# Reordering the seam between the two halves of a linear-attention layer: key copies, the key-value sum and an output block

## The chip, the cores and the metric

The kernel runs on one core of one Trainium2 chip. The metric is the device time of one launch in microseconds (us). The engines are TensorE (PE; its weight loads are shown apart as PEld), VectorE (DVE), ScalarE (ACT), GpSimd (POOL) and SyncE (SP), which here only issues transfers. Each runs its own instruction stream in order, and they meet at semaphores.

## The reference, cut to what matters

Two layers follow each other on `x` of shape (2, 2048, 512). The first is a gated state-space layer (Mamba) and takes the larger part of the time; the change doesn't touch it. The second is a linear attention with a feed-forward end:

```
xn  = layernorm(x)
q   = softmax(xn @ Wq + bq)            over the 64 features of each of 8 heads
k   = softmax(xn @ Wk + bk + mask)     over the 2048 tokens
v   = xn @ Wv + bv
att = sum over tokens of k (outer) v   one 64x64 matrix a head, for each batch row
y   = q @ att
h   = silu(layernorm(y) * (1 + scale) + shift)
out = x + h @ W_out + b_out
```

`att` of a batch row needs all of its keys and values. So nothing of `y` and `out` for the second batch row can be computed until the last block of keys and values of that row has been summed in.

## The kernel before, in words

The second layer works on 16 blocks of 256 tokens (two tiles of 128): blocks 0 to 7 are batch row 0, blocks 8 to 15 are batch row 1. Two pipelines run in one loop `for n in range(16)` that is written out by hand for each engine: the projections of block `n`, and from `n = 9` on also the output of block `K = n - 9` of batch row 0. After the loop the projections are over, and the output of blocks 7 to 15 remains. The stretch around the end of the loop is the one that changes.

The steps and the lines that the profile gives them:

- `q_mm`, `v_mm`, `k_mm`, `o_mm` (TensorE, all L435): products with 32-bit weights split in a high and a low part, 12 matmuls of 512 columns a tile for q, v and o. `o_mm(K)` makes the two tiles 2K and 2K+1 of the last product, called o12 and o13 for `K = 6`.
- `k_tr`, `q_tr` (TensorE, L480, L472): transposes of the exponentiated keys and queries. `k_evac` (ScalarE, 128x512, `arena_c<-ps,keep`) copies the two transposed key tiles out of PSUM with the mask, and `q_evac` (ScalarE, `arena_c<-ps`) the queries.
- `kv_mm(n)` (TensorE, L490, 16 matmuls) is the key-value sum of block n in one PSUM bank; it waits for both copies of `k_evac(n)`. `add_kv(n)` (VectorE, L1163, four instructions) adds it to the running sum and frees the bank. `k_sums` (L1171, L1173, L1175) closes the softmax's denominator, and `attention(1)` (L1184, four instructions) writes the attention matrix of batch row 1.
- `y_mm(K)` (TensorE, L500, two tiles, 16 matmuls). For `K >= 8` it waits for `attention(1)`. `y_block(K)` (VectorE): two scalings out of PSUM (L1196), the statistics (L1083) and their aggregation (L1088). `layer_rs` (GpSimd, L1306 to L1311) makes the scale and offset, `norm_h(K)` (ScalarE, two 128x512, `arena_b<-arena_b`) applies them.
- `h_tr(K)` (TensorE, L429, 8 transposes), `feat_h(K)` (ScalarE: four times a SiLU out of PSUM and a copy to `xh`), `lows` (VectorE, L1099, four subtractions to `xl`), then `o_mm(K)` and `finish(K)` (VectorE, L1208, one addition for each tile). `bias_rows(K)` (GpSimd, L1404) has added the output bias to the residual rows before. SyncE stores the result and loads the residual rows of a later block into the same buffer.

PSUM has 8 banks, given out in turn by `bank8`: each product takes the next bank and first waits until what held it before has been read. In the stretch at hand, by that turn, the banks of the steps are: o12 bank 2 (held before by the first half of `h_tr(6)`), o13 bank 3 (the second half of `h_tr(6)`), `kv_mm(15)` bank 4 (held before by `kv_mm(14)`), the halves of `h_tr(7)` banks 5 and 6 (the transposed keys of block 15), then y16 to y19 banks 7, 0, 1, 2, o14 bank 3 and o15 bank 4.

The feature buffers `xh`/`xl` come in three sets, and `f_bufs`, between SiLU and subtraction, in three.

Of the kernel before, what the change touches and what calls it, by code (L numbers as in the profile page):

```python
# [18 lines left out]
def program(nc, A, out):  # L19
# [12 lines left out]
    with ctx:  # L32
# [185 lines left out]
        def _(e):  # L218
# [135 lines left out]
            for s in range(NS + LAG + 3):  # L354
# [3 lines left out]
                if s < NS:  # L358
# [8 lines left out]
                    if c > 0 and (j, pr) in OUTM:  # L367
                        n, q0 = divmod(OUTM[j, pr], 8)
# [11 lines left out]
                    if (U, pr) in CPART:  # L380
                        i, n = CPART[U, pr]
# [32 lines left out]
            def bank8(key, release):  # L414
                i = order[nxt[0] % len(order)]
                nxt[0] += 1
                if held8[i] is not None:
                    e.wait_ge(*held8[i])
                held8[i] = release
                bank_of[key] = i  # L420
                return PS[i]

            def feat_tr(no, Z):
                for g in range(2):
                    P = bank8(("ft", no, g), (a_f, 4 * no + 2 * g + 2))
                    for q in range(2):
                        for n in range(2):
                            f = 2 * g + q
                            last = e.transpose(P[:, TB * q + 128 * n:TB * q + 128 * n + 128], Z[:, n, 128 * f:128 * f + 128], ident)  # L429
                    last.then_inc(p_ft)  # L430

            def product(P, lhs, rhs):
                for k in range(4):
                    for n, (a, b) in enumerate(((0, 0), (0, 1), (1, 0))):
                        last = e.matmul(P, lhs(a, k), rhs(b, k), start=(k == 0 and n == 0), stop=(k == 3 and n == 2))  # L435
                return last
# [31 lines left out]
            def q_tr(t):  # L468
                e.wait_ge(a_qe, t + 1)
                P = bank8(("qt", t), (a_qT, t + 1))  # L470
                for f in range(4):
                    last = e.transpose(P[:, 128 * f:128 * f + 128], q_bufs[t % 4][:, 128 * f:128 * f + 128], ident)  # L472
                last.then_inc(p_qt)
# [9 lines left out]
            def kv_mm(n):  # L483

                e.wait_ge(a_E, 2 * n + 2)
                e.wait_ge(v_v, 2 * n + 2)
                P = bank8(("kv", n), (v_ac, n + 1))
                for f in range(4):
                    for t in (2 * n, 2 * n + 1):
                        last = e.matmul(P[:, 128 * f:128 * f + 128], E_bufs[t % 4][:, 128 * f:128 * f + 128],  # L490
                                        vv[:, t % 4, 128 * f:128 * f + 128], start=(t % 2 == 0), stop=(t % 2 == 1))
                last.then_inc(p_kv)
# [10 lines left out]
            def h_tr(K):  # L503
                e.wait_ge(a_nx, 2 * h_no(K) + 2)
                feat_tr(h_no(K), x_bufs[2 + K % 2])

            def o_mm(K):
                ht = t_bufs[h_no(K) % 3]
                e.wait_ge(v_lo, 4 * h_no(K) + 4)
                e.wait_ge(v_wl, 8)  # L510
                for n in range(2):
                    P = bank8(("o", 2 * K + n), (v_o, 2 * K + n + 1))
                    product(P, lambda a, kk: ht[a][:, kk, 128 * n:128 * n + 128], W("o")).then_inc(p_o)

# [3 lines left out]
            for n in range(16):  # L518
                K = n - 9
# [24 lines left out]
            k_tr(15)  # L544
            y_mm(7)
            q_tr(31)
            o_mm(6)
            kv_mm(15)
            h_tr(7)
            y_mm(8)  # L550
            y_mm(9)
# [10 lines left out]
        def _(e):  # L562
            def act(o_, i_, f, **kw):
                return e.activation(o_, i_, f, **kw)  # L564
# [246 lines left out]
            def norm_h(K):  # L811
                norm(h_no(K), x_bufs[2 + K % 2])
# [31 lines left out]
            def feat_h(K):  # L844
                b = K // 8
                feat(h_no(K), lambda f: g2[:, f, b:b + 1], lambda f: b2[:, f, b:b + 1], ACT.Silu)
# [5 lines left out]
            def q_evac(t):  # L852
                at_ = 128 * (t % 18)
                e.wait_ge(p_qt, t + 1)
                if t >= 18:
                    e.wait_ge(p_ya, t - 17)
                act(qT[:, :, at_:at_ + 128], PS[bank_of["qt", t]].rearrange("p (a b) -> p a b", a=4), ACT.Identity).then_inc(a_qT)
# [40 lines left out]
            for n in range(16):  # L898
                K = n - 9
# [24 lines left out]
                if K >= 0:  # L924
                    feat_h(K)
                    if n < 15:
                        e.preload_act_table_set("natural_log_exp_and_others")
            norm_h(7)
            k_evac(15)
            q_evac(31)  # L930
            feat_h(7)
            norm_h(8)
            norm_h(9)
# [7 lines left out]
        def _(e):  # L941
# [85 lines left out]
            for s in range(NS):  # L1027
# [10 lines left out]
                if (U, pr) in ((62, 14), (63, 4)):  # L1038
                    n = 2 + U - 62
# [54 lines left out]
            def lows(no):  # L1094
                hi, lo = t_bufs[no % 3]
                for f in range(4):
                    i = 4 * no + f
                    e.wait_ge(a_fh, i + 1)
                    e.tensor_tensor(lo[:, f, :], f_bufs[i % 3], hi[:, f, :].bitcast(f32), SUB).then_inc(v_lo)  # L1099
# [53 lines left out]
            def add_kv(n):  # L1153

                P = PS[bank_of["kv", n]]
                e.wait_ge(p_kv, n + 1)
                if n % 8 == 0:
                    e.tensor_scalar(flat(acc), P, 1.0, None, MUL).then_inc(v_ac)
                else:
                    e.wait_ge(a_fc, n)  # L1160
                    e.wait_ge(v_ac, n)
                    for f in range(4):
                        last = e.scalar_tensor_tensor(acc[:, f, :], acc[:, f, :], fac[:, n, f:f + 1], P[:, 128 * f:128 * f + 128],  # L1163
                                                      MUL, ADD)
                    last.then_inc(v_ac)
# [11 lines left out]
            def attention(b):  # L1177
                e.wait_ge(v_ac, 8 * b + 8)
                e.wait_ge(v_ks, 4 * b + 4)
                e.wait_ge(g_att, 3)  # L1180
                if b:
                    e.wait_ge(p_ya, 16)
                for f in range(4):
                    e.scalar_tensor_tensor(att[:, f, :], acc[:, f, :], ks[:, f:f + 1], bm, MUL, MUL).then_inc(v_att)  # L1184

            def y_block(K):
                yt = x_bufs[2 + K % 2]
                if K >= 2:
                    e.wait_ge(p_ft, 2 * h_no(K - 2) + 2)
                else:  # L1190
                    e.wait_ge(v_wl, 8)
                e.wait_ge(v_rq, 2 * K + 2)
                for n in range(2):
                    t = 2 * K + n
                    e.wait_ge(p_ya, t + 1)
                    e.tensor_tensor(yt[:, n, :].rearrange("p (a b) -> p a b", a=8),  # L1196
                                    PS[bank_of["y", t]].rearrange("p (a b) -> p a b", a=8),
                                    rq[:, t, :].unsqueeze(2).broadcast_to([128, 8, 64]), MUL).then_inc(v_y)
                e.wait_ge(v_y, 2 * K + 2)
                layer_norm(h_no(K), yt)  # L1200

            def finish(K):
                for n in range(2):
                    t = 2 * K + n
                    O = o_bufs[xo_buf(K, n)]
                    e.wait_ge(p_o, t + 1)
                    e.wait_ge(g_xo, t + 1)
                    e.tensor_tensor(O, PS[bank_of["o", t]], O, ADD).then_inc(v_o)  # L1208
# [19 lines left out]
            for n in range(16):  # L1228
                K = n - 9
                if n < 15:  # L1230
                    norm_x(n + 1)
                if n >= 2:
                    add_kv(n - 2)
                if n == 9:
                    attention(0)
                q_part(2 * n)
                v_part(2 * n)
                if n == 8:
                    k_sums(0)
                if K >= 0:  # L1240
                    y_block(K)
                k_part(n, 0)
                if n == 15:
                    k_part(n, 1)
                sum_part(2 * n)
                if K >= 1:
                    finish(K - 1)
                if n < 15:
                    lows(feat_no(n + 1))
                if n == 3:  # L1250
                    for h in range(2):
                        split_o(h)
                q_part(2 * n + 1)
                v_part(2 * n + 1)
                if n < 15:
                    k_part(n, 1)
                sum_part(2 * n + 1)
                if K >= 0:
                    lows(h_no(K))
            add_kv(14)  # L1260
            y_block(7)
            k_sums(1)
            finish(6)
            add_kv(15)
            attention(1)
            lows(h_no(7))
            y_block(8)
            y_block(9)
# [433 lines left out]
```

## Time and profile before

| | us |
|---|---|
| median of 3 runs | 2419.46 (2418.34 to 2419.83) |
| the profiled execution's own time | 2415.44 |
| its span, first to last instruction | 2413.7 |
| TensorE busy | 2229.7 (92%) |
| VectorE busy | 2165.5 (90%) |
| GpSimd busy | 1916.4 (79%) |
| ScalarE busy | 1679.5 (70%) |

Times inside the trace are us from the start of the span. The second layer's projections begin near 1933, its loop ends near 2323 and the last output rows are made near 2410. In a timeline, a row gives start, duration, engine, line, what is written and read, the number of instructions merged in it, and in brackets the engine's idle time before it with what ended that. The ends of matmuls are modelled, so starts are the better measure on TensorE.

### The profile page before, as it was taken

The numbers are of one execution on the slowest core, as the hardware profiler recorded it, in microseconds if no ns is written. First come the engines' busy times: TensorE is split into PE (matmuls) and PEld (weight loads), VectorE is DVE, ScalarE is ACT, GpSimd is POOL, SyncE is SP. The second block draws the span as 40 slices with busy tenths as digits, with TensorE's granted clock in tenths as the row PEclk, the third lists the DMA queues.
The fourth block names the chain that finished last, engine by engine and source line by source line (L and its number), as shares of the span: only waits on it lengthen the run. The fifth ranks groups of instructions, "written<-read, shape, count | busy, mean of one in ns | idle before, by whom it ended". The sixth has DMA issues, their size and how long they took to land. (4 is left out here: it accounts for less than half of the span.)

```text
span 2413.7 us, 24243 instructions
## 1 busy us (share of the span) xinstructions
PE 2229.7 (92%) x6954; PEld 1151.1 (48%) x6954; DVE 2165.5 (90%) x2363; ACT 1679.5 (70%) x3268; POOL 1916.4 (79%) x1250
## 2 busy tenths in 40 slices
PE   9898999989998999899889998998987899999989
PEld 3233334334433443344334333433433388988878
DVE  4898999999999999999999999999999966666666
ACT  3677777877787778778877877787555455466655
POOL 0789999999999999999999999999987722232225
PEclk9999999999999999999999999999998999999999
DMA  6510231032004110411041023003100121011113
GB/s 228 203 61 26 74 132 35 31 131 75 31 31 158 44 35 27 159 57 65 19 174 44 31 75 131 27 31 129 60 31 20 65 77 34 26 56 58 49 53 123
DMA packets 78050, 176.10 MB, mean 73 GB/s; under 512 B 7453, under 2 KB 10781, under 8 KB 77918
## 3 DMA queue, kind: packets, MB, share of 16 engines
q1 hardware_dynamic: 77918, 174.56, 21.4%
q8 instruction: 56, 0.92, 0.1%
q14 instruction: 76, 0.62, 0.1%
HBM read 157.23 MB, written 17.30 MB: 72 GB/s over the span
## 5 line engine op out<-in xcount | busy, mean ns | idle before, releaser
L1379 POOL TENSOR_TENSOR arena<-arena 128x1024 f32<-128x1024 f32 x512 | 1198.9, 2358 | 106.7 <-ACT arena L564 73.5
L984 DVE TENSOR_TENSOR_SCAN arena<-ps,arena 128x512 f32<-128x512 f32 x1024 | 1237.7, 1249 | 0.8 <-ACT ps L564 0.6
L564 ACT ACTIVATE ps<-arena 128x512 f32<-128x512 f32 x1087 | 723.7, 681 | 370.4 <-DVE arena L984 298.2
L307 PE MATMUL ps<-arena,keep 128*128 128x512 f32 x1770 | 861.3, 617 | 119.8 <-POOL arena L1379 91.9
L972 DVE TENSOR_TENSOR arena<-ps,arena 128x1024 f32<-128x1024 f32 x512 | 615.1, 1201 | 19.3 <-PE ps L307 11.7
L307 PEld LDWEIGHTS ps<-arena,keep 128*128 128x128 f32 x1770 | 331.5, 194 | 599.3 <-issue 339.3
L253 PE MATMUL ps<-arena 128*128 128x512 f32 x1024 | 460.4, 593 | 0.7 <-ACT arena L564 0.7
L253 PEld LDWEIGHTS ps<-arena 128*128 128x128 f32 x1024 | 194.6, 191 | 247.8 <-issue 247.3
L564 ACT ACTIVATE arena<-arena 128x2 f32<-128x2 f32 (+2 forms) x599 | 227.5, 383 | 23.5 <-POOL arena L1339 12.2
L293 PE MATMUL ps<-arena 128*128 128x512 f32 x512 | 233.3, 597 | 0.0
L1339 POOL TENSOR_TENSOR arena<-arena 128x512 f32<-128x512 f32 x168 | 213.3, 1271 | 10.1 <-ACT arena L564 2.1
L1384 POOL TENSOR_TENSOR arena<-arena 128x512 f32<-128x512 f32 x139 | 177.3, 1276 | 10.9
L564 ACT ACTIVATE arena<-ps 128x512 f32<-128x512 f32 (+2 forms) x273 | 138.5, 516 | 65.2 <-PE ps L253 22.8
L564 ACT ACTIVATE arena<-ps,keep 128x509 f32<-128x509 f32 (+3 forms) x240 | 167.7, 699 | 22.7 <-PE ps L253 12.5
L1397 POOL TENSOR_TENSOR arena_c<-arena_c 128x512 f32<-128x512 f32 x32 | 33.4, 1044 | 167.2 <-DVE arena_c L1139 166.0
L293 PEld LDWEIGHTS ps<-arena 128*128 128x128 f32 x512 | 98.4, 192 | 124.3 <-issue 124.1
L1306 POOL TENSOR_SCALAR arena_b<-arena_b 128x2 f32<-128x2 f32 x32 | 8.2, 257 | 151.4 <-DVE arena_b L1088 151.3
L564 ACT ACTIVATE arena_c<-arena_c 128x256 f32<-128x256 f32 (+3 forms) x112 | 54.9, 493 | 74.9 <-POOL arena_c L1397 48.4
L303 PE MATMUL ps<-arena 128*128 128x512 f32 x128 | 72.7, 651 | 37.0 <-DVE arena L990 35.9
L564 ACT ACTIVATE arena_b<-ps,keep 128x256 f32<-128x256 f32 x128 | 70.9, 554 | 49.8 <-PE ps L429 40.3
L1099 DVE TENSOR_TENSOR xl<-arena_b,xh 128x256 fp32r<-128x256 f32 x128 | 57.5, 468 | 45.9 <-ACT xh L564 45.1
L1111 DVE SCALAR_TENSOR_TENSOR arena_c<-ps,keep,arena_b 128x256 f32<-128x256 f32 x64 | 28.0, 480 | 65.5 <-PE ps L435 65.5
(146 smaller groups left out, 2697.8 us busy)
## 6 DMA issues: line engine op xcount, KB each, us to landing
arena<-scr_bc SPq DMA_DIRECT2D x128, 512.0 KB, 6.4
arena<-in_inT SPq DMA_DIRECT2D x128, 256.0 KB, 2.6
arena<-in_x SPq DMA_DIRECT2D x17, 512.0 KB, 4.1
scr_x<-arena SPq DMA_DIRECT2D x32, 256.0 KB, 2.0
arena_b<-scr_x SPq DMA_DIRECT2D x16, 512.0 KB, 3.7
arena_c<-scr_x SPq DMA_DIRECT2D x32, 256.0 KB, 2.9
out<-arena_c SPq DMA_DIRECT2D x32, 256.0 KB, 2.0
arena<-in_x SPq DMA_DIRECT2D x30, 256.0 KB, 3.5
```

Source lines behind the costliest of these rows:

```text
L253: last = e.matmul(P, W[:, q, :], xnT[c % 2][:, q, :], start=(q == 0), stop=(q == 3))
L293: e.matmul(P, u[c % 2][:, q, 128 * n:128 * n + 128], wout[:, q, :], start=(c == NCH - 1 and q == 0 or parts and q == 6), stop=(q == 7 or p ...
L303: e.matmul(YP, dg[U % 2], u[c % 2][:, j, :], start=True, stop=False)
L307: last = e.matmul(YP, ident, hb[G % R][:, i, :], start=False, stop=(g == NG - 1 and i == n - 1))
L564: return e.activation(o_, i_, f, **kw)
L972: e.tensor_tensor(hb[G % R], DU.unsqueeze(1).broadcast_to([128, GN, T]), Bt[:, GN * g:GN * g + GN, :], MUL).then_inc(v_tt)
L984: e.tensor_tensor_scan(H, DA[s % 4], H, h0, MUL, ADD).then_inc(v_sc)
L1099: e.tensor_tensor(lo[:, f, :], f_bufs[i % 3], hi[:, f, :].bitcast(f32), SUB).then_inc(v_lo)
L1339: e.tensor_tensor(v, v, tp[:, w, :], ADD).then_inc(g_tap)
L1379: m_ = e.tensor_tensor(H, H, Ct[:, GN * g:GN * g + GN, :], MUL)
L1384: m_ = e.tensor_tensor(H[:, 0, :], H[:, 0, :], H[:, 1, :], ADD)
L1397: e.tensor_tensor(Q3, Q3, m8[t % 4].unsqueeze(2).broadcast_to([128, 8, 64]), SUB).then_inc(g_q)
```

## The change

The arithmetic is the same; four places in the written-out order at the end of the loop differ. TensorE: the key-value sum of block 15 stands between the two tiles of output block 6 and no longer behind both. ScalarE: the copies of the last keys and queries stand ahead of the normalisation of block 7. VectorE: `y_block(7)` comes before `add_kv(14)`, and `finish(6)` comes behind `attention(1)`.

```diff
@@ block.tensor
-            def o_mm(K):
+            def o_mm(K, tiles=(0, 1)):
                 ht = t_bufs[h_no(K) % 3]
                 e.wait_ge(v_lo, 4 * h_no(K) + 4)
                 e.wait_ge(v_wl, 8)
-                for n in range(2):
+                for n in tiles:
                     P = bank8(("o", 2 * K + n), (v_o, 2 * K + n + 1))
@@
             k_tr(15)
             y_mm(7)
             q_tr(31)
-            o_mm(6)
+            o_mm(6, (0,))
             kv_mm(15)
+            o_mm(6, (1,))
             h_tr(7)
             y_mm(8)
             y_mm(9)
@@ block.scalar
-            norm_h(7)
             k_evac(15)
             q_evac(31)
+            norm_h(7)
             feat_h(7)
             norm_h(8)
             norm_h(9)
@@ block.vector
+            y_block(7)
             add_kv(14)
-            y_block(7)
             k_sums(1)
-            finish(6)
             add_kv(15)
             attention(1)
+            finish(6)
             lows(h_no(7))
             y_block(8)
             y_block(9)
```

With the new order on TensorE, `kv_mm(15)` takes bank 3 (held before by the second half of `h_tr(6)`), and o13 takes bank 4 (held before by `kv_mm(14)`).

## Rows read from the trace of the kernel before

**Rows 1.** Waits of TensorE from 2352 on: total us, times, longest us.

```profile
PE ps L435 <- DVE xl L1099: 2.5, 1, 2.5
```

**Rows 2.** The chain that ended last: start us, us, what.

```profile
2339.01 1.29 DVE arena_b L1196 x2
...
2347.13 1.26 ACT arena_b L564 x2
```

**Rows 3.** Timeline of TensorE, 2324 to 2353.

```profile
2324.05 0.50 PE L435 MATMUL ps<-wh_o,xh 128*128 128x512 f32 x1 [0.48 <-DVE xl L1099]
...
2326.95 0.39 PE L435 MATMUL ps<-wh_o,xh 128*128 128x512 f32 x1
...
2332.31 2.05 PE L490 MATMUL ps<-arena_c 128*128 128x128 f32 x16 [2.48 <-ACT arena_c L564]
2334.19 1.04 PE L429 MATMUL ps<-keep,arena_b 128*128 128x128 f32 x8
2336.75 3.84 PE L500 MATMUL ps<-arena_c 128*128 128x128 f32 x32 [1.52 <-DVE arena_c L1184]
...
2345.91 1.04 PE L429 MATMUL ps<-keep,arena_b 128*128 128x128 f32 x8
...
2352.10 0.50 PE L435 MATMUL ps<-wh_o,xh 128*128 128x512 f32 x1 [2.50 <-DVE xl L1099]
```

**Rows 4.** Timeline of TensorE: `kv_mm(13)`, then the first matmuls of q30 and v30.

```profile
2290.09 1.95 PE L490 MATMUL ps<-arena_c 128*128 128x128 f32 x16
2291.79 0.48 PE L435 MATMUL ps<-wh_q,xh 128*128 128x512 f32 x1
...
2294.63 0.39 PE L435 MATMUL ps<-wh_v,xh 128*128 128x512 f32 x1
```

**Rows 5.** Timeline of ScalarE, 2329 to 2348.

```profile
2329.59 1.52 ACT L564 ACTIVATE arena_b<-arena_b 128x512 f32<-128x512 f32 x2 [6.05 <-POOL arena_b L1311]
2331.01 1.24 ACT L564 ACTIVATE arena_c<-ps,keep 128x512 f32<-128x512 f32 x2
2332.15 0.59 ACT L564 ACTIVATE arena_c<-ps 128x512 f32<-128x512 f32 x1
...
2346.41 1.52 ACT L564 ACTIVATE arena_b<-arena_b 128x512 f32<-128x512 f32 x2 [1.24 <-POOL arena_b L1311]
```

**Rows 6.** Timeline of VectorE, 2323 to 2339.

```profile
2323.91 1.11 DVE L1163 SCALAR_TENSOR_TENSOR arena_c<-arena_c,ps 128x128 f32<-128x128 f32 x4
2324.95 1.28 DVE L1196 TENSOR_TENSOR arena_b<-ps,arena_c 128x512 f32<-128x512 f32 x2
...
2327.75 0.16 DVE L1171 TENSOR_TENSOR arena_c<-arena_c 128x32 f32<-128x32 f32 x1
...
2334.39 1.12 DVE L1163 SCALAR_TENSOR_TENSOR arena_c<-arena_c,ps 128x128 f32<-128x128 f32 x4 [3.84 <-PE ps L490]
2335.55 1.14 DVE L1184 SCALAR_TENSOR_TENSOR arena_c<-arena_c 128x128 f32<-128x128 f32 x4
...
2338.66 0.42 DVE L1099 TENSOR_TENSOR xl<-arena_b,xh 128x256 fp32r<-128x256 f32 x1 [0.48 <-ACT xh L564]
```

**Rows 7.** Timeline of GpSimd: `bias_rows(7)`.

```profile
2329.51 2.50 POOL L1404 TENSOR_TENSOR arena_c<-arena_c,arena_b 128x512 f32<-128x512 f32 x2
```

**Rows 8.** A later `bias_rows` on GpSimd and a subtraction of `lows` beside it.

```profile
2364.22 2.70 POOL L1404 TENSOR_TENSOR arena_c<-arena_c,arena_b 128x512 f32<-128x512 f32 x2
...
2364.54 1.26 DVE L1099 TENSOR_TENSOR xl<-arena_b,xh 128x256 fp32r<-128x256 f32 x1 [0.41 <-ACT xh L564]
```

**Rows 9.** Timeline of TensorE, first layer: four matmuls behind a stall, twice.

```profile
209.53 1.98 PE L307 MATMUL ps<-arena,keep 128*128 128x512 f32 x4 [2.96 <-POOL arena L1379]
...
232.17 3.48 PE L307 MATMUL ps<-arena,keep 128*128 128x512 f32 x4 [2.66 <-POOL arena L1379]
```

**Rows 10.** Windows there: stretch, length, PE busy, granted clock, DMA share, GB/s.

```profile
209.50:212.50 3.00, 2.98 (x7) 1.00 0.02 5
...
232.20:235.60 3.40, 3.40 (x5) 0.56 0.00 0
```

## The prediction

> **What bounds the kernel now.** I read the windows of equal length first, to find the stretch that the change touches, then the waits of TensorE, the chain that ended last, and the timeline of each engine from 2320 to 2352. In the second layer TensorE is the engine that sets the time: from 2352 to the end its list of waits has one entry, the 2.5 us that ends at 2352.10 [rows 1], and behind it stands nothing but its own work. So the time of the whole kernel follows the start of the matmuls at 2352.10, the first tile of output block 8 (o16). Whatever moves that start moves the end by as much. The question is what sets it.
>
> The timeline of TensorE shows three long stalls ahead of that point [rows 3]: 2.48 us before `kv_mm(15)` (until 2332.31), 1.52 us before `y_mm(8)` (until 2336.75), and 2.50 us before o16. The reader should see that the third isn't caused by anything near it. Back from 2352.10 the chain goes through `feat_h(8)` and `norm_h(9)` on ScalarE, GpSimd's `layer_rs`, and `y_block(9)` and `y_block(8)` on VectorE, which start at 2339.01 [rows 2]. `y_block(8)` starts there because `lows(7)` stands ahead of it in VectorE's order; its last subtraction runs from 2338.66 to 2339.08 [rows 6]. Those wait for `feat_h(7)`, which waits for the transposes of `h_tr(7)` at 2334.19, and these stand in TensorE's queue behind `kv_mm(15)` [rows 3]. `kv_mm(15)` waits for the copies of the last keys (2331.01, 1.24 us), and these stand in ScalarE's queue behind `norm_h(7)`, which waited 6.05 us for its statistics until 2329.59 [rows 5].
>
> From `h_tr(7)` at 2334.19 to o16 at 2352.10 are 17.91 us, of which the first 4.89 (to the end of the last subtraction) are the chain of `feat_h(7)` and the rest, 13.02, is VectorE, GpSimd and ScalarE in series. TensorE isn't in it, as long as `y_mm(8)` and `y_mm(9)` come in time. So the gain is the shift of `h_tr(7)`, if both halves of that sentence hold.
>
> **Part 1: ScalarE.** The copies of the keys no longer wait for `norm_h(7)`. They can start when `feat_h(6)` is through, at the latest when VectorE's last subtraction of that block is, 2323.9 [rows 6]. Two copies take 1.24 and the query copy 0.59 [rows 5]: the keys are out of PSUM by 2325.1, the queries by 2325.7. `norm_h(7)` has its scale no sooner than 2328.5 (part 3), so it isn't delayed by them: cost 0, hidden in ScalarE's old 6.05 us of idle time. Without that cover it would be their 1.8 us.
>
> **Part 2: TensorE.** o12 starts at 2324.05, as before, since all that it waits for is ahead of the change in each order. Its 12 matmuls take until 2326.95 [rows 3]. The keys being there since 2325.1, `kv_mm(15)` starts with no stall. It costs 1.70 from its first matmul to the next product's, by `kv_mm(13)` at 2290.09 followed at 2291.79, and a 12-matmul product behind such a change takes 2.84, 2291.79 to 2294.63 [rows 4]. So: 2326.95 + 1.70 + 2.84 = 2331.49 for the start of `h_tr(7)`, against 2334.19: **2.70 us earlier**. It is no more work than before; the stall of 2.48 goes, and the other 0.2 is what the first matmuls after a stall take longer.
>
> The added wait is the bank. o13 now needs bank 4, which `kv_mm(14)` held and `add_kv(14)` frees. On VectorE `add_kv(14)` now stands behind `y_block(7)`, which is part 3: free at about 2327.8, wanted at 2328.65, so 0.8 us to spare.
>
> **Part 3: VectorE.** Before, `add_kv(14)` from 2323.91, `y_block(7)` from 2324.95, `k_sums` from 2327.75 [rows 6]. The two trade places, with nothing to wait for (y14 and y15 are made by TensorE before o12): `y_block(7)` starts at 2323.91, 1.04 sooner, `add_kv(14)` follows at 2326.7 and is through at 2327.8, `k_sums` starts at 2327.75 as before. `norm_h(7)` started 4.64 behind `y_block(7)` (2329.59 against 2324.95), so it starts at 2328.55 and ends at 2330.07 [rows 5, 6]. `h_tr(7)` wants it at 2331.49: 1.4 to spare. In the old order it would have ended at 2331.11, still 0.4 early, so the swap by itself is worth 0 by this sum.
>
> `add_kv(15)` started 2.08 behind `kv_mm(15)` (2334.39 against 2332.31) [rows 3, 6]: now 2329.03. `attention(1)` is 1.16 behind it: 2330.19, and `y_mm(8)` could start 1.20 behind that, at 2331.39. TensorE gets to it 0.87 behind `h_tr(7)`, at 2332.36. So the stall of 1.52 goes too, with 1.0 to spare. `finish(6)` behind it: two additions of 0.7, o12 then o13, done by 2332.7. It frees bank 2 for y19 (wanted at about 2335) and banks for o15; `lows(7)` begins at 2333.2, so it isn't in the way. What SP hangs on it (two stores of block 6, then two loads of block 8) comes some 3 us later, and `bias_rows(8)`, the reader, stands behind a `layer_rs` that comes only after o16. Cost 0.
>
> **Part 4: a port.** `attention(1)` now falls beside `bias_rows(7)`, which started 4.56 behind `y_block(7)` (2329.51) and will run from 2328.47 to 2330.97 [rows 6, 7]. Nothing ran beside it before. The nearest row: a subtraction of `lows` that started beside a `bias_rows` took 1.26 where one by itself took 0.42, and the GpSimd pair took 2.70 for 2.50 [rows 6, 8]. So `attention(1)`, whose instructions also read two tensors of SBUF, may be held until 2330.97 and end at 2332.1 and not at 2331.3. `y_mm(8)` then starts at 2332.2, still under the 2332.36. Lower bound 0; upper bound a hold of both GpSimd instructions, 2.5 us, so `y_mm(8)` 1.3 late; value taken 0.8 on VectorE, 0 on TensorE. The Trainium skill has this rule ("SBUF — State Buffer", Who interferes with whom): a VectorE instruction with two SBUF inputs and a GpSimd instruction that reads SBUF exclude each other for the whole instruction. By it the hold is certain, by the row likely; the sum is the same by both, with 0.1 to spare and not 1.0.
>
> **Behind `h_tr(7)`.** The last subtraction of `lows(7)` ends 4.89 behind 2331.49, at 2336.38. `y_mm(8)` and `y_mm(9)` run 2332.36 to 2336.2 (3.84 [rows 3]), o14 starts at about 2336.4 with a stall of some 0.3, and o14 and o15 (5.6) end at 2342.0. `norm_h(9)` ended at 2347.93 [rows 5] and now ends at 2345.23; then `h_tr(9)`, 1.04 [rows 3], is over at 2346.3, and TensorE has nothing until o16 at 2352.10 - 2.70 = 2349.40. **The third stall doesn't go, it grows from 2.50 to about 3.1.**
>
> **The sum.** Removed on the path 2.70, added 0: the profiled execution's own time goes from 2415.44 to 2412.74. That execution lies 4.02 below the median of the runs shown, 2419.46; taken off there, 2416.8, which is 0.11% less. What a measurement of this kernel can tell from no change is about 0.2%, 4.8 us. So the forecast is a real gain that is too small to be told.
>
> **Rivals.**
>
> *The clock falls in the longer stall.* Forecast 3.1 us of idle TensorE. In this trace a stall of 2.50 didn't cost the clock (the 0.50 of the first matmul at 2352.10 is that of a product started at the full 2.4 GHz), nor did one of 2.96 (granted 1.00 after it, four matmuls in 1.98), but one of 2.66 did: granted 0.56, so mostly 1.2 GHz, four matmuls in 3.48 [rows 3, 9, 10]. The price by these rows is 3.48 - 1.98 = 1.5, and it lies on the path, since o16 and all behind it is TensorE's own work. Time: 2416.8 + 1.5 = 2418.3. For it: 3.1 is longer than either of the first layer's two. Against it: of the two, the longer was the harmless one, so length alone doesn't decide. The Trainium skill ("TensorE: Matmul & The Clock Gate", Part 1) says that the throttled state is the default, which activity lifts, and that where the change falls varies between runs of one kernel; this trace agrees in that 2.96 kept the clock and 2.66 lost it. By it, some executions would have the fall and others not. Chance 0.25.
>
> *The port holds longer.* Both GpSimd instructions win over `attention(1)`: `y_mm(8)` 1.3 late, o14 0.7 late, and the first subtraction of `lows(7)` late by so much that the third buffer of `feat_h(7)` is waited for, about 0.3 on the path. Time 2417.1. Against it: the row shows a hold of one instruction. Chance 0.05.
>
> *The bank takes the stall's place, and it gets slower.* o13 waits for `add_kv(14)` behind `y_block(7)`. It decides once `y_block(7)` is over 0.8 late: from there each us is one on the path, and from 3.5 late (0.8 + 2.7) the kernel is slower than before; a `y_block(7)` 4.5 late would give 2420.5. For it: VectorE's order is fixed, and the wait is new. Against it: all that `y_block(7)` reads is done about a microsecond before 2323.91. Chance 0.02.
>
> *Nothing comes through.* The chain behind `h_tr(7)` has a second root that isn't seen, as a transfer or GpSimd, and o16 stays at 2352.10: 2419.5. Against it: each link of it follows the one before within tenths. Chance 0.05.
>
> **How the numbers follow.** Forecast 0.60, clock 0.25, port 0.05, bank 0.02, nothing 0.05, and 0.03 for what I don't see. The runs of before lie within 1.5 us, and the profiled one 4.0 below the median, so scatter adds to each. The forecast's own range is 2415.3 to 2418.3. The upper end of the whole is that of no gain with 0.5 of scatter, 2420.0, the lower is the forecast less 3.0 of scatter, 2413.8. Faster by over 0.2% needs 2.1 more than the forecast has, which only scatter gives: 0.06. Slower by over 0.2% needs the bank over 8 us late or scatter: 0.03. The rest, 0.91, is within.
>
> **What the profile would show.** Right: `kv_mm(15)` near 2326.95 with no wait, o13 behind it with no wait, `h_tr(7)` near 2331.5, no stall before `y_mm(8)`, a short one before o14, `y_block(8)` near 2336.3, o16 near 2349.4 behind a stall of about 3.1 by `xl`; `attention(1)` as long as 1.9 beside L1404. Wrong: a stall at the head of o13 (the bank), at `y_mm(8)` (the port), an o16 that hasn't moved, or one that has, with first matmuls of 0.8 and a granted clock near 0.5 behind it.

## The result and the profile after

The changed kernel takes 2414.46 us (median of 20 runs, 2412.47 to 2416.60), the kernel before 2418.57 in its 20 (2415.65 to 2420.62). The ratio is 0.9985 with a 95% interval of 0.9978 to 0.9991, so 2.2 to 5.3 us less. The forecast was 2.7 less. 2414.46 lies in the whole stated range (2413.8 to 2420.0), but 0.8 below the forecast's own (2415.3 to 2418.3), in the part that was allowed for scatter. The gain is smaller than the 0.2% that I had called the limit of what can be told, but 20 runs did tell it from nothing. Three executions of two of the variants below ran at a mean granted clock of 0.65 from end to end and took 3248 to 3268 us; no comparison uses them.

The timeline of TensorE after the change, same stretch as [rows 3] (start us, us, engine, line, what, idle before and its releaser):

```profile
2323.76 0.50 PE L435 MATMUL ps<-wh_o,xh 128*128 128x512 f32 x1 [0.48 <-DVE xl L1100]
...
2326.64 1.95 PE L490 MATMUL ps<-arena_c 128*128 128x128 f32 x16
...
2331.16 1.04 PE L429 MATMUL ps<-keep,arena_b 128*128 128x128 f32 x8
2332.03 3.74 PE L500 MATMUL ps<-arena_c 128*128 128x128 f32 x32
2336.11 0.50 PE L435 MATMUL ps<-wh_o,xh 128*128 128x512 f32 x1 [0.34 <-DVE xl L1100]
...
2342.17 1.09 PE L429 MATMUL ps<-keep,arena_b 128*128 128x128 f32 x8 [0.32 <-ACT arena_b L565]
...
2349.06 0.50 PE L435 MATMUL ps<-wh_o,xh 128*128 128x512 f32 x1 [3.03 <-DVE xl L1100]
```

The stalls before `kv_mm(15)` and `y_mm(8)` are gone, small ones stand before o14 (0.34) and `h_tr(8)` (0.32), and the one before o16 has grown from 2.50 to 3.03. The starts are to be read against o12, since what lies ahead of o12 is unchanged and yet varies: in the thirteen profiles of this study that are compared here, o12 starts between 2322.8 and 2325.8. From o12 to o16 it was 2352.10 - 2324.05 = 28.05 us [rows 3] and is 2349.06 - 2323.76 = 25.30. So the profile gives a gain of 2.75.

VectorE, the rows that answer to [rows 6]:

```profile
2323.62 1.28 DVE L1197 TENSOR_TENSOR arena_b<-ps,arena_c 128x512 f32<-128x512 f32 x2
...
2326.43 1.09 DVE L1164 SCALAR_TENSOR_TENSOR arena_c<-arena_c,ps 128x128 f32<-128x128 f32 x4
2327.43 0.18 DVE L1172 TENSOR_TENSOR arena_c<-arena_c 128x32 f32<-128x32 f32 x1
...
2328.62 1.12 DVE L1164 SCALAR_TENSOR_TENSOR arena_c<-arena_c,ps 128x128 f32<-128x128 f32 x4 [0.55 <-PE ps L490]
2329.78 1.88 DVE L1185 SCALAR_TENSOR_TENSOR arena_c<-arena_c 128x128 f32<-128x128 f32 x4
2331.59 1.27 DVE L1209 TENSOR_TENSOR arena_c<-ps,arena_c 128x512 f32<-128x512 f32 x2
2332.92 0.43 DVE L1100 TENSOR_TENSOR xl<-arena_b,xh 128x256 fp32r<-128x256 f32 x1
```

`attention(1)` (L1185 now) takes 1.88 where it took 1.14: the first of its four instructions takes 1.09, each of the others 0.34. On ScalarE the copies come first (`k_evac`, `q_evac`, then `norm_h(7)`), and on GpSimd `bias_rows(7)` covers the start of `attention(1)`:

```profile
2323.15 1.25 ACT L565 ACTIVATE arena_c<-ps,keep 128x512 f32<-128x512 f32 x2
2324.29 0.60 ACT L565 ACTIVATE arena_c<-ps 128x512 f32<-128x512 f32 x1
2328.26 1.52 ACT L565 ACTIVATE arena_b<-arena_b 128x512 f32<-128x512 f32 x2 [3.37 <-POOL arena_b L1312]
```

```profile
2328.18 2.54 POOL L1405 TENSOR_TENSOR arena_c<-arena_c,arena_b 128x512 f32<-128x512 f32 x2
```

### The profile page after: what moved, and what is told of

Its sections match the earlier page's. It is cut to its first block and busy times, and to the rows that moved or that the text cites. A ratio compares the mean times of both kernels' runs of the same rounds, so it can differ in the third digit from the quotient of the medians.

```text
span 2410.7 us, 24244 instructions
## 1 busy us (share of the span) xinstructions
PE 2229.8 (92%) x6954; PEld 1151.9 (48%) x6954; DVE 2166.1 (90%) x2363; ACT 1679.6 (70%) x3268; POOL 1916.5 (80%) x1250
```

## The experiments

Three things were open. Which of the three edits makes the gain, does the clock fall in the stall that has grown, and what is the longer `attention(1)`? For each kernel I read two distances from the first product of o12: that to o16, which holds all that the seam does, and that from o16 to the next `y_mm`, the two tiles of output block 8, which is 5.58 us at full clock.

### One edit alone

ScalarE's edit alone, on the kernel before:

```diff
-            norm_h(7)
             k_evac(15)
             q_evac(31)
+            norm_h(7)
             feat_h(7)
```

> Only the ScalarE part of the change. Measure: distance from the first matmul of o12 to the first of o16, 28.05 us before and 25.31 after the whole change. Theory A (the key copies behind norm_h(7) were the one cause, and the other two parts only move waits that are hidden): the key-value sum follows o13 without a stall at +5.6, h_tr(7) at +7.4, y_mm(8) stalls by about 1.8 because attention ends late, but lows(7) is done in time, so the distance is 25.3 to 25.6 and the time 2.5 to 2.7 below before, as with the whole change. Theory B (the three parts are needed together, because a late y_mm(8) and a late attention push lows(7) and o14): distance 26.3 to 27.2, 0.9 to 1.7 us gained.

Measured: 2414.85 us, ratio 0.9986 (0.9977 to 0.9995), as much as the whole change.

```profile
2325.12 0.50 PE L435 MATMUL ps<-wh_o,xh 128*128 128x512 f32 x1 [0.48 <-DVE xl L1099]
...
2330.70 1.95 PE L490 MATMUL ps<-arena_c 128*128 128x128 f32 x16
2332.48 1.04 PE L429 MATMUL ps<-keep,arena_b 128*128 128x128 f32 x8
2335.03 3.84 PE L500 MATMUL ps<-arena_c 128*128 128x128 f32 x32 [1.52 <-DVE arena_c L1184]
...
2350.40 0.62 PE L435 MATMUL ps<-wh_o,xh 128*128 128x512 f32 x1 [2.51 <-DVE xl L1099]
...
2357.58 1.95 PE L500 MATMUL ps<-arena_c 128*128 128x128 f32 x16
```

o12 to o16 is 25.28. The key-value sum stays behind both tiles and has no stall (2330.70 is 5.58 behind o12), and `h_tr(7)` comes at +7.36 against +7.40 in the whole change. The stall of 1.52 before `y_mm(8)` is still there and costs nothing: TensorE works it off inside the time that the chain through VectorE, GpSimd and ScalarE takes anyway. Theory A holds, B falls. The next product after o16 comes at +7.18, not +5.58; that is for the clock, below.

VectorE's edit alone:

```diff
+            y_block(7)
             add_kv(14)
-            y_block(7)
             k_sums(1)
-            finish(6)
             add_kv(15)
             attention(1)
+            finish(6)
```

> Only the VectorE part. y_block(7) is 1.04 sooner, so norm_h(7), the key copies, the key-value sum and h_tr(7) are 1.04 sooner. Theory A: finish(6) behind attention(1) makes lows(7) start late, as its third buffer is waited for, which gives back 0.8 of it: distance from o12 to o16 27.8, gain 0.2 to 0.3. Theory B (the order of finish(6) is hidden): 27.0, gain 1.0.

Measured: 2417.38 us, ratio 0.9998 (0.9989 to 1.0007), no difference that can be told. o12 to o16 is 27.66: theory A. `h_tr(7)` came at +9.11, 1.03 sooner, and 0.64 of that was lost again: `lows(7)` now begins behind `finish(6)`, as the rows of the kernel without TensorE's move show below.

TensorE's edit alone:

```diff
-            o_mm(6)
+            o_mm(6, (0,))
             kv_mm(15)
+            o_mm(6, (1,))
```

> Only the TensorE part. The copies of the last keys are still behind norm_h(7), so the key-value sum, now in the middle of block 6, stalls until the same moment as before (o12 + 8.3), and o13 with all behind it comes after it. h_tr(7) at +12.8 instead of +10.1. finish(6) in front of add_kv(15) waits for o13 too. Theory A: slower than before by 2.7 to 3.2 us, distance from o12 to o16 30.8 to 31.2. Theory B (o13 fills some idle time whatever the order): no change, 28.0.

Measured: 2421.60 us, ratio 1.0018 (1.0009 to 1.0026), slower.

```profile
2322.83 0.50 PE L435 MATMUL ps<-wh_o,xh 128*128 128x512 f32 x1 [0.48 <-DVE xl L1100]
...
2331.08 3.78 PE L490 MATMUL ps<-arena_c 128*128 128x128 f32 x16 [5.24 <-ACT arena_c L565]
...
2337.48 1.04 PE L429 MATMUL ps<-keep,arena_b 128*128 128x128 f32 x8
2340.63 5.46 PE L500 MATMUL ps<-arena_c 128*128 128x128 f32 x32 [2.11 <-DVE arena_c L1185]
...
2356.34 0.50 PE L435 MATMUL ps<-wh_o,xh 128*128 128x512 f32 x1 [1.23 <-DVE xl L1100]
```

The sum waits until the same +8.25 (+8.26 before), and o13, which used to fill that time, now comes behind it. The stall is 5.24 and not 2.48. Theory A had the sign and the mechanism; its size, 30.8 to 31.2, was too small against 33.51. The rest is the clock. It fell twice: behind the stall of 5.24 the 16 matmuls of the sum took 3.78 where they take 1.95, and behind the stall of 2.11 the `y_mm` pair took 5.46 where it takes 3.84. The windows of the first fall are the stall, granted 0.71 on average, and the sum behind it, 0.50:

```profile
2325.80:2331.00 5.20, 0.04 (x1) 0.71 0.13 50
2331.00:2334.00 3.00, 2.92 (x13) 0.50 0.00 0
```

### Two edits of the three

Without the move on TensorE (the kernel after, with `o_mm(6)` whole and `kv_mm(15)` behind it):

> The ScalarE and VectorE parts, the key-value sum back behind both tiles of output block 6. Theory A': the sum runs at +5.6, so add_kv(15) and attention(1) end at about +10.0; finish(6), now behind them, ends at +11.4, and lows(7) begins there and not at +9.2. The third buffer between SiLU and subtraction then comes free 1.0 late, so the distance from o12 to o16 is 26.3, a gain of 1.7 and less than that of the ScalarE part alone. Theory B (more parts, more gain; the move on TensorE is what the order of VectorE doesn't matter to): 25.3 to 25.6, a gain of 2.5 to 2.7.

Measured: 2415.97 us, ratio 0.9991 (0.9982 to 1.0000), o12 to o16 25.92. It is between the two theories, nearer to A': the loss against ScalarE's part alone is 0.64 and not 1.0. The mechanism shows in the rows of VectorE and ScalarE. `finish(6)` stands between `attention(1)` and the subtractions, which then come three in a row, and the last SiLU on ScalarE waits 0.53 for its buffer, a wait that neither the kernel before nor the kernel after has:

```profile
2334.52 1.14 DVE L1184 SCALAR_TENSOR_TENSOR arena_c<-arena_c 128x128 f32<-128x128 f32 x4
2335.58 1.28 DVE L1208 TENSOR_TENSOR arena_c<-ps,arena_c 128x512 f32<-128x512 f32 x2
2336.78 1.09 DVE L1099 TENSOR_TENSOR xl<-arena_b,xh 128x256 fp32r<-128x256 f32 x3
2338.28 0.43 DVE L1099 TENSOR_TENSOR xl<-arena_b,xh 128x256 fp32r<-128x256 f32 x1 [0.41 <-ACT xh L564]
```

```profile
2337.23 0.56 ACT L564 ACTIVATE arena_b<-ps,keep 128x256 f32<-128x256 f32 x1 [0.53 <-DVE xl L1099]
```

Without VectorE's reorder (the kernel after, with the six calls on VectorE in their old order):

> The TensorE and ScalarE parts without VectorE's. The key-value sum runs at o12 + 2.9, but add_kv(15) stands behind finish(6), which waits for o13, the tile that the sum was moved ahead of: attention ends at +10.9, the stall before y_mm(8) is about 2.6 and lows(7) starts 0.4 late. Theory A: distance from o12 to o16 25.7, gain 2.3 over before, 0.4 less than the ScalarE part alone. Theory B (the move on TensorE helps once the copies are early): 25.3, gain 2.7.

Measured: 2413.17 us, ratio 0.9981 (0.9972 to 0.9990), o12 to o16 26.27. The distance is 0.6 over theory A. The sum is early (2325.74), but its addition waits on VectorE behind `finish(6)`, which waits for o13:

```profile
2330.46 0.69 DVE L1209 TENSOR_TENSOR arena_c<-ps,arena_c 128x512 f32<-128x512 f32 x1 [2.71 <-PE ps L435]
2331.07 1.11 DVE L1164 SCALAR_TENSOR_TENSOR arena_c<-arena_c,ps 128x128 f32<-128x128 f32 x4
```

`y_mm(8)` stalled for 2.11 (2.6 forecast), and the clock fell there in this execution:

```profile
2333.42 5.47 PE L500 MATMUL ps<-arena_c 128*128 128x128 f32 x32 [2.11 <-DVE arena_c L1185]
...
2344.20 1.04 PE L429 MATMUL ps<-keep,arena_b 128*128 128x128 f32 x8
...
2349.12 0.50 PE L435 MATMUL ps<-wh_o,xh 128*128 128x512 f32 x1 [1.23 <-DVE xl L1100]
```

The pair of `y_mm` took 5.47 and not 3.84, so TensorE came to `h_tr(8)` (2344.20) at +21.35, where it was at +19.08 with ScalarE's edit alone. o16 is 4.92 behind it, about what o14 is behind `h_tr(7)` in the whole change (4.95). So here TensorE's own lateness is in the chain to o16: `feat_h(8)` on ScalarE waited 0.36 for `h_tr(8)`, where in the whole change and with ScalarE's edit alone it follows `norm_h(9)` at once. The order by itself costs little: the last subtraction of `lows(7)` starts at +11.93, against +11.83 with ScalarE's edit alone. So of the 0.99 between 26.27 and 25.28, about 0.1 is the order and 0.9 the fall (an estimate from these rows), and theory A had the order too dear. o16 itself ran at full clock behind a stall of 1.23.

The median of this kernel is the lowest of the study, though its profile has a longer way to o16 than the whole change; its interval overlaps those of the whole change and of ScalarE's edit alone, so no order among the three is shown. The differences of 0.6 and 1.0 in these distances are from one profile each. TensorE's and VectorE's edits without ScalarE's, the third pair, weren't run.

### The clock in the stall before o16

The whole change once more, unaltered, for its profile:

> The changed kernel itself, once more, for the clock behind the stall of 3.0 us. Theory A (the fall depends on where the stall lies in time, not on its length): the distance from o12 to o16 is 25.3 again, and the block of o16 and o17 takes either 5.6 us (no fall) or 6.9 to 7.2 (a fall). Theory B (this kernel keeps the clock always): 5.6.

```profile
2324.38 0.50 PE L435 MATMUL ps<-wh_o,xh 128*128 128x512 f32 x1 [0.48 <-DVE xl L1100]
...
2349.71 0.79 PE L435 MATMUL ps<-wh_o,xh 128*128 128x512 f32 x1 [3.03 <-DVE xl L1100]
...
2356.71 1.95 PE L500 MATMUL ps<-arena_c 128*128 128x128 f32 x16
```

The windows before and behind that start (stretch, length, PE busy, granted clock, DMA share, GB/s), first of this execution, then of the first profile of the same kernel:

```profile
2346.60:2349.70 3.10, 0.08 (x1) 0.94 0.51 154
2349.70:2352.70 3.00, 2.99 (x7) 0.50 0.07 24
2352.70:2356.70 4.00, 4.00 (x18) 0.99 0.00 0
```

```profile
2346.00:2349.00 3.00, 0.04 (x1) 1.00 0.49 144
2349.00:2352.00 3.00, 2.94 (x13) 1.00 0.10 38
```

Same kernel, same stall of 3.03, and 25.33 from o12 to o16 against 25.30; one execution kept 2.4 GHz, the other ran at 1.2 GHz (0.50) for some 3 us, and its two tiles took 7.00 and not 5.58. So theory B is out. The length of the stall didn't decide between these two; that its place in time did, as theory A has it, isn't shown. Over all the profiles with this stall left empty:

| kernel | stall before o16, us | o16 to next `y_mm`, us | clock |
|---|---|---|---|
| before | 2.50 | 5.58 | kept |
| after, first profile | 3.03 | 5.58 | kept |
| after, again | 3.03 | 7.00 | fell |
| ScalarE's edit alone | 2.51 | 7.18 | fell |
| ScalarE's and VectorE's | 3.03 | 6.91 | fell |
| VectorE's edit alone | 3.03 | 7.17 | fell |
| `bias_rows(7)` early | 3.03 | 5.59 | kept |

Four of seven fell, at a price of 1.3 to 1.6, and 2.51 was enough. With VectorE's edit alone the fall came only within o16, whose first matmuls ran at full clock. The kernel before has the stall of ScalarE's edit alone (2.50 and 2.51), so a fall there is likely in some of its executions too; its one profile kept the clock, so that isn't shown. Whether half a microsecond makes the fall more frequent, seven profiles can't say. Shorter stalls went both ways as well: behind the 2.11 before `y_mm(8)` the clock fell in two profiles (TensorE's edit alone, and the whole change without VectorE's), and behind 2.10 and 2.11 before o16 it held in the two kernels of the last experiment.

Then the stall filled. The whole change with matmuls that compute nothing that is used, into the bank that o16 overwrites:

```diff
                 if K < 15:
                     h_tr(K + 1)
+                if K == 8:
+                    i = order[nxt[0] % len(order)]
+                    e.wait_ge(*held8[i])
+                    for j in range(12):
+                        e.matmul(PS[i], t_bufs[h_no(7) % 3][0][:, j % 4, 0:128], WH["o"][:, j % 4, :], start=True, stop=True)
                 o_mm(K)
```

> The changed kernel with 12 matmuls of 512 columns added on TensorE between h_tr(9) and o16, on data that is there already, into the bank that o16 then overwrites. They take 0.32 + 11 x 0.228 = 2.8 us and lie in the stall of 3.0 us that ends at o16, so by themselves they cost nothing. Theory A (in some executions the granted clock falls in that stall, and o16 then starts at half speed, 1.3 to 1.6 us lost): o16 at full speed in the profile, y20-to-o16 distance as in the changed kernel, and a median 0.5 to 1.5 us below that of the changed kernel. Theory B (the fall is rare or is the profile's): same median as the changed kernel within 0.3 us. Slower by over 0.3 us would mean that they don't fit.

Measured: 2414.04 us, ratio 0.9984 (0.9975 to 0.9992); o12 to o16 25.34, the block 5.58.

ScalarE's edit alone with ten such matmuls:

> The ScalarE part alone, and 10 matmuls of 512 columns in its stall of 2.5 us before o16. In its profile the clock fell there and the block of o16 and o17 took 7.2 us, not 5.6. Theory A (the fall is common in that stall, and activity prevents it): 5.6 in the profile, distance from o12 to o16 25.3, median 0.5 to 1.6 us below that of the ScalarE part alone. Theory B (rare): the medians agree within 0.4 us.

Measured: 2413.81 us, ratio 0.9985 (0.9976 to 0.9993); o12 to o16 25.32, the block 5.57:

```profile
2349.93 0.50 PE L435 MATMUL ps<-wh_o,xh 128*128 128x512 f32 x1 [0.23 <-DVE xl L1104]
...
2355.50 1.95 PE L500 MATMUL ps<-arena_c 128*128 128x128 f32 x16
```

The filling costs nothing that these runs can show, and both profiles keep the clock. The medians are 0.4 and 1.0 below those of the kernels with the stall empty, 2414.46 and 2414.85, in the direction of theory A; the first misses its 0.5 to 1.5, the second is inside. But the ratios differ by 0.0001 with intervals of 0.0017, so a gain in time from it isn't shown. By the ratios theory B (rare, or the profile's) isn't excluded. That activity in the stall prevents the fall fits all profiles, but isn't shown: three of seven kept the clock with the stall empty, and at that rate two filled ones keep it by chance about one time in five (3/7 squared, 0.18).

### The port

The whole change, with `bias_rows(7)` ahead of `layer_rs(7)` on GpSimd:

```diff
-            layer_rs(h_no(7))
             bias_rows(7)
+            layer_rs(h_no(7))
             layer_rs(h_no(8))
```

> The changed kernel with bias_rows(7) on GpSimd ahead of layer_rs(7) and so no longer beside attention(1). Theory A (a shared port: GpSimd's instruction holds VectorE's for its whole length): the four instructions of attention(1) take 1.14 us again, where they took 1.88 in the changed kernel, finish(6) starts 0.7 sooner. TensorE's stalls stay as they are, as y_mm(8) was not held, so the time is that of the changed kernel within 0.3 us. Theory B (the 0.7 has another cause, such as the copies on ScalarE): 1.88 again.

Measured: 2415.19 us, ratio 0.9990 (0.9981 to 0.9999). The median is 0.7 over that of the whole change and not within 0.3, but the intervals overlap. The rows are from another execution of the same kernel:

> A second look at the changed kernel with bias_rows(7) ahead of layer_rs(7), for its profile. Theory A (the port): attention(1), four instructions, 1.14 us and not 1.88; the distance from o12 to o16 stays 25.3. Theory B: 1.88 again.

```profile
2330.24 1.12 DVE L1164 SCALAR_TENSOR_TENSOR arena_c<-arena_c,ps 128x128 f32<-128x128 f32 x4 [0.56 <-PE ps L490]
2331.39 1.14 DVE L1185 SCALAR_TENSOR_TENSOR arena_c<-arena_c 128x128 f32<-128x128 f32 x4
2332.45 1.28 DVE L1209 TENSOR_TENSOR arena_c<-ps,arena_c 128x512 f32<-128x512 f32 x2
```

`attention(1)` takes 1.14 again, `y_mm(8)` starts where it did, at +8.29 from o12 (+8.27), and o12 to o16 is 25.34: theory A in the profile, with nothing gained or lost there. What moved along is the collision itself. `bias_rows(7)` now lies beside the subtractions of block 6, and the first of them takes 1.52 where one by itself takes 0.42; the last still starts 0.48 before o12, as in the whole change, so this costs nothing either.

### The stall that is left

Since o16 waits on a chain that begins with `h_tr(7)`, I tried to shorten the chain: `feat_h(8)` before `norm_h(9)`, and `h_tr(9)` between the two tiles of output block 8.

```diff
 # ScalarE
             norm_h(8)
-            norm_h(9)
             feat_h(8)
+            norm_h(9)
 # TensorE, loop over K
+                if K == 8:
+                    o_mm(8, (0,))
+                    h_tr(9)
+                    o_mm(8, (1,))
+                    continue
```

> The changed kernel with the second half of the seam reordered too: ScalarE takes feat_h(8) ahead of norm_h(9), and TensorE puts h_tr(9) between the two tiles of output block 8. o16 then waits for h_tr(8) + 4.9 and no longer for norm_h(9): 2.0 us sooner than in the changed kernel, behind a stall of 2.1 and not 3.0. But h_tr(10) then waits for norm_h(10), which stands behind feat_h(9) on ScalarE: about 1.0 us of new stall, and o18 comes 0.5 us sooner. Theory A: 0.5 us below the changed kernel, to 2.0 if the shorter stall keeps the clock. Theory B (the next stall takes all of it): no change or slower by up to 0.5.

Measured: 2415.60 us, ratio 0.9988 (0.9979 to 0.9998). o16 came at +23.39, 1.9 sooner, with a stall of 2.10 before it. But o18 came at +35.00 where it was at +33.45 in the whole change, so the profile lost 1.55. The waits named a cause that neither theory had:

```profile
PE ps L435 <- DVE xl L1105: 2.9, 3, 2.1
PE ps L435 <- DVE arena_c L1214: 1.8, 1, 1.8
```

L1214 is `finish`. With `h_tr(9)` between the tiles, the turn of the banks gives o18 the bank of o16, and `finish(8)` that frees it stands behind `y_block(11)` on VectorE. With `finish(8)` put ahead of `y_block(11)`:

> The reordered second half of the seam again, with finish(8) ahead of y_block(11) on VectorE, so that o18 finds its bank free: it waited 1.8 us for it. Theory A: o18 at o12 + 33.1 (35.0 before this edit, 33.4 in the changed kernel), so 1.9 us below the first try and 0.3 below the changed kernel. Theory B (the wait moves to lows(9), which ran beside bias_rows(8) in 3.5 us, or to the next bank): 33.5 or more, no gain over the changed kernel.

Measured: 2414.16 us, ratio 0.9985 (0.9976 to 0.9994). o18 starts at 2357.55, +33.08 from o12 at 2324.47, as theory A had it, and the 1.8 is gone. That is 0.37 sooner than the +33.45 of the whole change, and the time can't tell the two apart. Of the 1.86 that o16 comes sooner (+23.44 against +25.30), 0.8 goes to the transposes of `h_tr(9)`: they used to lie in front of a stall, beside other engines' work, and now stand between two products that wait for nothing. Another 0.5 goes to `h_tr(10)`, which now comes 2.28 and not 1.78 behind the `y_mm` before it, since it waits for `norm_h(10)`.

## Why the prediction was right, point by point

- *The time follows o16.* Right. From o16 to the end of the span it is 61.6 us in both profiles (2413.7 - 2352.10 and 2410.7 - 2349.06).
- *Part 2: `h_tr(7)` 2.70 sooner.* Right, from o12 it is +7.40 against +10.14, so 2.74. The bank cost nothing, as forecast: `add_kv(14)` was through at 2327.52 and o13 started at 2328.34 with no wait, 0.8 to spare.
- *Part 1: the copies cost nothing.* Right as a cost, wrong as an account of the gain. I put the 2.70 down to TensorE's part and priced ScalarE's as a permission for it. ScalarE's edit alone gives all of it (o12 to o16 in 25.28), TensorE's alone loses (33.51). My chain names the root rightly, the copies behind `norm_h(7)`; the step that failed is that I added the parts up only in the one order of the diff. With early copies, the sum follows o13 with no stall, and the same three products in either order end at the same time.
- *The stall before `y_mm(8)`: "goes too".* It went, but it was worth nothing: with 1.52 of it left, o16 comes as early. The prediction did say that TensorE isn't in the chain behind `h_tr(7)`, but didn't draw this from it.
- *Part 3: the swap is worth 0, finish(6) costs 0.* Right in the whole change, though close: `finish(6)` ended at 2332.86 and `lows(7)` began at 2332.92, where I had 0.5 between them, since the port took the room. In other company the order of `finish(6)` is worth something: behind `attention(1)` it costs 0.64 when the sum comes late (25.92 against 25.28), and ahead of it, with the sum in the middle, it waits for o13 and leaves a stall of 2.11 before `y_mm(8)`, which cost 0.99 in its one profile, nearly all of it by the clock. So on top of ScalarE's edit the TensorE and VectorE edits need each other, and as a pair they are worth about nothing (25.30 against 25.28).
- *Part 4: the port.* Right, 0.74 longer against 0.8 taken, hidden as forecast; moving GpSimd's work away took it back to 1.14. The hold was that of one instruction, 1.09 for the first of four, which ended within 0.2 of `bias_rows(7)`; `add_kv(15)` ran beside the same `bias_rows(7)`, with one input in PSUM, and took its usual 1.12. The rule of the Trainium skill ("SBUF — State Buffer", Who interferes with whom), that a VectorE instruction with two SBUF inputs contends with a GpSimd instruction that reads SBUF, agrees with both.
- *What is left.* Stall before o14 0.34 (forecast 0.3), before o16 3.03 (3.1), the start of o16 at +25.30 (+25.35).
- *The clock rival.* The fall exists and its price was right (1.3 to 1.6, taken 1.5). Its chance of 0.25 was too small for single executions: it isn't in the first profile, but in four of the seven with that stall. Its time was too high: at 2418.3 it lies above all 20 runs of the changed kernel (2416.60 at most). The rival charged the fall to the kernel after alone, taking the 2.50 of the kernel before as safe because one execution kept its clock; if both fall about as often, little of it is left in the difference, but how often the kernel before falls isn't known. The Trainium skill's remark that the point where the clock changes varies between runs of one kernel ("TensorE: Matmul & The Clock Gate", Part 1) agrees with the two profiles of the changed kernel, 5.58 and 7.00.
- *The size.* Forecast 2.7, measured 3.6 by the ratio with 2.2 to 5.3 around it (the medians differ by 4.1). The profile says 2.75, and the forecast lies inside the interval. The median came 2.3 below the forecast's, of which 0.9 is that the kernel before itself came out at 2418.57 and not 2419.46; the rest isn't explained, and is smaller than the scatter of 3 us in the start of o12. That the absolute time fell inside the stated range is in part luck: it hung on a base of three runs and on the 3.0 allowed for scatter.

## What to carry to other kernels

When a change has edits on several in-order engines, work out each one alone and in pairs, not only all of them together: here one moved line on ScalarE made the gain, and the other two edits on top of it only paid for each other. A stall on the busiest engine is worth something only if the chain that ends last goes through it, so look for what the engine would wait for next before you count its removal. When two products change places, follow the turn of the buffers: the new tenant inherits another engine's order, and that wait (1.8 us here) isn't seen in the lines that were moved.

## What the runs showed of the hardware

TensorE lost the clock behind a stall of 2.11 us before `y_mm(8)` in two profiles, behind one of 2.51 before o16 in one, and behind stalls of 3.03 before o16 in three; it kept it behind 3.03 in two, one of them of the same kernel as a profile that lost it. Before o16 the loss was 1.3 to 1.6 us each time. One profile of a kernel therefore says little about whether its stalls are harmless. A reorder can be paid twice: behind a stall of 5.24 the 16 matmuls of the sum took 3.78 us instead of 1.95. And a VectorE instruction with both inputs in SBUF took 1.09 us instead of 0.34 beside a GpSimd addition on SBUF, where one with an input in PSUM took its usual time.
